# A graph transformer block: the product of probabilities and values, split into two matmuls of 64 columns

## The reference

```
q = q.reshape(B, T, H, HD) * HD ** (-0.5)
...
att = jax.nn.softmax(jnp.einsum('bthd,bshd->bhts', q, k), axis=-1)
o = jnp.einsum('bhts,bshd->bthd', att, v).reshape(B, T, D)
```

## Time and profile before

| | |
|---|---|
| runs of the kernel | 1949.89 and 1949.10 us, median 1949.49 |
| profiled execution, span from the first to the last instruction | 1945.8 us |
| instructions in it | 30993 |
| TensorE busy | 1816.8 us, 93% |
| VectorE busy | 1184.2 us, 61% |
| ScalarE busy | 722.9 us, 37% |
| attention stage, products of probabilities and values | from 499.8 to 1664.1 us |

### The profile page before, as it was taken

The page is one execution under the profiler, slowest core; times in us unless marked ns, Lnnn a source line. Parts: engine busy times, 40 slices in busy tenths (PEclk is TensorE's granted clock), DMA queues, the critical chain, the costliest instruction groups (busy, mean ns, idle before and its releaser), DMA issues.

```text
span 1945.8 us, 30993 instructions
## 1 busy us (share of the span) xinstructions
PE 1816.8 (93%) x10495; PEld 1626.1 (84%) x10495; DVE 1184.2 (61%) x2343; ACT 722.9 (37%) x1346; POOL 337.8 (17%) x335
## 2 busy tenths in 40 slices
PE   2999989987899999999999999989999999899998
PEld 1788567855899999999889898889999999787996
DVE  7776568775566546663756747656566666675332
ACT  1223201014555445445544553245555444220110
POOL 3210001002112112020101003100000013565440
PEclk9999999988899999999999999999999999999999
DMA  3101001011021100030000000000000002111111
GB/s 109 33 7 44 11 11 33 1 48 44 12 118 33 28 28 6 1 123 12 12 6 12 12 1 17 23 11 12 6 12 6 7 1 68 51 59 44 44 33 53
DMA packets 24782, 58.00 MB, mean 30 GB/s; under 512 B 2537, under 2 KB 4805, under 8 KB 24013
## 3 DMA queue, kind: packets, MB, share of 16 engines
q1 hardware_dynamic: 24650, 56.18, 8.9%
HBM read 44.87 MB, written 11.30 MB: 29 GB/s over the span
## 4 chain that ended last, share of the span: by engine, by line
PE 85%; DVE 7%; issue 2%; DMA 2%; DVEq 1%; POOL 1%; ACT 1%; SPq 0%; POOLq 0%; ACTq 0%
PE ps L2284 21%; PE ps L2169 13%; PE ps L2339 7%; PE ps L2227 6%; PE ps L2266 6%; PE ps L2270 6%; PE ps L1961 6%; PE ps L2368 4%; PE ps L2055 3%; PE ps L2092 3%; PE ps L1974 1%; PE ps L2295 1%; DVE share L1729 1%; DMA tok_a<-in_x 1%; DVE max_part L1712 1%
## 5 line engine op out<-in xcount | busy, mean ns | idle before, releaser
L2284 PE MATMUL ps<-p_raw,v_ones 125*128 125x250 f32 x2080 | 526.8, 375 | 9.7 <-DVE feat L1731 6.2
L1712 DVE TENSOR_REDUCE max_part<-ps 125x2 f32<-125x500 f32 x520 | 330.3, 674 | 213.6 <-PE ps L2227 203.2
L1288 ACT ACTIVATE p_raw<-ps 125x500 f32<-125x500 f32 x520 | 304.1, 586 | 332.0 <-PE ps L2270 327.5
L2284 PEld LDWEIGHTS ps<-p_raw,v_ones 125*128 125x128 f32 x2080 | 360.9, 190 | 36.2 <-issue 7.7
L1729 DVE RECIPROCAL share<-ps 64x250 f32<-64x250 f32 x120 | 206.2, 1718 | 86.1 <-PE ps L2284 83.5
L2266 PE MATMUL ps<-q_both_a,k_both_a 128*125 128x250 f32 x520 | 183.8, 374 | 1.8 <-issue 0.9
L2266 PE MATMUL ps<-q_both_b,k_both_b 128*125 128x250 f32 x520 | 181.7, 371 | 0.0
L1552 DVE TENSOR_SCALAR onehot<-iota_h,win_key,key_t 125x320 f16 x453 | 172.2, 380 | 0.7 <-issue 0.6
L892 POOL CAST w_hi<-w_raw 128x512 fp32r<-128x512 f32 x44 | 28.3, 642 | 816.7 <-issue 351.8
L2169 PE MATMUL ps<-xa_hi,w_hi 128*128 128x418 f32 (+1 forms) x448 | 151.1, 337 | 13.4 <-POOL w_lo L894 9.1
L1551 DVE TENSOR_SCALAR onehot<-iota_h,low_t 125x125 f16 x453 | 124.4, 275 | 57.8 <-PE ps L2092 29.2
(11 more groups left out here) (378 smaller groups left out, 3399.2 us busy)
## 6 DMA issues: line engine op xcount, KB each, us to landing
w_raw<-in_w_mlp SPq DMA_DIRECT2D x32, 256.0 KB, 2.6
w_raw<-in_w_gps SPq DMA_DIRECT2D x16, 256.0 KB, 2.6
w_raw<-in_w_tp SPq DMA_DIRECT2D x16, 256.0 KB, 2.6
w_raw<-in_w_sp SPq DMA_DIRECT2D x12, 256.0 KB, 2.6
w_raw<-in_w_cr SPq DMA_DIRECT2D x12, 256.0 KB, 2.6
d_xt<-xb_hi SPq DMA_DIRECT2D x1, 2508.0 KB, 7.4
d_xt<-xb_lo SPq DMA_DIRECT2D x1, 2508.0 KB, 14.9
xa_hi<-d_xt SPq DMA_DIRECT2D x1, 2508.0 KB, 9.7
```

The source lines that it names most:

```text
L1288: act.activation(p_raw[:, g % PR, :], ps[0:TOK, g % 2, 0:4 * TOK], ACT.Exp, scale=SCALE).then_inc(s_exp, 1)
L1712: dve.tensor_reduce(part[:, y, :, j], ps[0:TOK, bank, 0:4 * TOK].rearrange("p (h k) -> p h k", h=2), AX.X, ALU.max)\
L2284: ins = pe.matmul(ps[:, bank, 0:2 * TOK], v_ones[:, n % 2, kt, h:h + 2, :], p_raw[:, g % PR, cols], start=(b == 0 and x == 0), stop=last)
```

## The change

Each matmul of `product` becomes two. The first takes the group `h` as 64 columns and writes partitions 0 to 63 of the bank, the second the group `h + 1` and writes partitions 64 to 127. Both read the same 250 columns of `p_raw`. Each half starts and ends its own sum; the semaphore is raised by the last matmul, as before.

```
-                    ins = pe.matmul(ps[:, bank, 0:2 * TOK], v_ones[:, n % 2, kt, h:h + 2, :], p_raw[:, g % PR, cols], start=(b == 0 and x == 0), stop=last)
+                    for y in range(2):
+                        ins = pe.matmul(ps[64 * y:64 * y + 64, bank, 0:2 * TOK], v_ones[:, n % 2, kt, h + y, :], p_raw[:, g % PR, cols],
+                                        start=(b == 0 and x == 0), stop=last)
                 ins.then_inc(s_pv, 1)
```

## The result

The changed kernel takes 2110.61 us (2109.42 to 2111.81) against 1949.49: ratio 1.0831, 95% interval 1.0811 to 1.0852, so it is slower by 161 us. The forecast was 2250 us, with a range of 2100 to 2570: the direction held and the time lies in the range, but it lies where the rival "perfect overlap with excursions" stood (2105), not at the forecast itself.

A forecast was written before the change was run, and what follows sets the result against it. TensorE was taken to bound the kernel. Per product, 0.28 us for passes and 0.32 for changing width make 0.60, times 518 is 311 us; less 10 us of waits, from 1949.49 this gave 2250 us, range 2100 to 2570.

The forecast's parts named there:

- perfect overlap with excursions: Rival for the product: halves run fully side by side, each change of width costs 0.32 us; 2105 us, chance 0.09.
- 4 T: Lower bound of a product's passes: each half makes four passes of T = 0.21 us, both halves side by side.
- the staircase: Forecast case: a product's halves overlap only partly, in five pass times, 1.06 us; with excursions, chance 0.52.
- What bounds the kernel: Attention stage: TensorE sets the pace, busy 1197.11 of 1240 us; what is added to it is added to the time.
- Part 1, the passes: In each product, twice as many passes over half the columns: body from 0.85 to 1.13 us, +0.28.
- The allowance for late loads: In a product, first passes in a just freed half may wait for their weight load: 0 to 0.15 us, 0.07 taken.
- Part 2, the excursion: Around products, going from full-width matmuls into a half and out again: 0.32 us each, 518 times.
- The row that spoke against it: L2238, a transpose with 33 active columns between full-width matmuls, showed no standing still before or after.
- The sum: Whole kernel: 0.60 us a product, 518 times, 311 us, less 10 us for waits on max_col and feat; 2250 us.
- halves one after the other: Rival for the product: eight passes in turn, 1.70 us, plus excursions; 2545 us, chance 0.23.
- Not slower: Rival: excursions free for 64 columns, halves side by side all the time; product stays 0.85 us, kernel 1950 us, chance 0.05.
- The granted clock falls: Possible upward correction: clock at 0.95 instead of 0.99 makes some 1500 us of work 4% longer, +60 us; no own chance.

## Why the prediction was right, and where not

The direction and the range held; the central figure did not. 2250 us was 139 us too much, and the time lies near the lower end of the range (2100), which was set by the bound of 4 T. The case that came true, pairs from the first pass on with excursions, had a chance of 0.09, against 0.52 for the staircase.

*What bounds the kernel*: right. TensorE set the pace before and does so now; the other engines' busy times did not move, and the products now last from 499.9 to 1826.5 us, 162 us longer than before.

*Part 1, the passes*: wrong in its term of +0.28 us a product; it measured 0. Three things stood in it. That a narrower pass is no cheaper held: 1.90 us for eight in one half. That halves overlap held too; it was called an assumption there. The step that failed is "the two passes of one matmul use the same half, so they follow each other; the first pass of the upper half can start only beside the second of the lower half". It took the order of issue for the order of start across both halves. The run that issues one half wholly ahead of the other shows that this order binds within a half alone, so the body stays at the lower bound, 4 T. The allowance for late loads in it (0.07) fell away with the staircase; only the first load shows, and that was in the excursion's price already (the +0.06 above).

*Part 2, the excursion*: right in mechanism and in size. 0.32 was forecast from the bias row L1964; 0.34 is read from the trace of the changed kernel, and 0.311 is left of it in the time, 0.31 to 0.32 in three more kernels with 260, 520 and 976 excursions. The row that spoke against it was rightly set aside: the transpose was the exception.

The Trainium skill's rule on a change of the tiling mode ("TensorEngine Tiling (Array Packing)", Key Properties) is borne out by these runs: a change between full width and halves costs TensorE's time, 0.34 us for both ways, and going from one half to the other within a product costs nothing that the steps of 0.21 us show. Of the Trainium skill's "TensorE: Matmul & The Clock Gate", Part 3, the trace agrees that two column groups run together (1.07 us for eight passes); its statement that matmuls start and end strictly in program order doesn't fit the time of the run with one half issued ahead of the other, which is 1.07 us too.

*The sum*: 518 x (0 + 0.34) = 176 us, less some 15 us that came back, is the 161 us measured. The prediction took 10 us off for the waits on max_col and feat. Those two went from 7.9 and 6.2 only to 7.9 and 4.5; what came back came from elsewhere, so this term was short by some 5 us and stood in the wrong place. That the rival's 2105 comes within 6 us of the time is in part luck: its excursion was 0.02 too cheap, 10 us in all, and half of that is made up by what it took off too little.

*The rivals*: "halves one after the other" is out by 434 us, and the run with both in one half shows what it would have been (2529.52 measured, 2545 worked out). "Not slower" needed excursions that are free for 64 columns; the only narrow form that these runs show to be free is the float32 transpose with 33. "The granted clock falls" didn't happen: 0.99 in the stage.

## What to carry to other kernels

Splitting a full-width matmul into column halves gained nothing here, since both halves together do what one pass did, and each trip from full width into halves and back cost 0.34 us, 0.31 to 0.32 after what came back elsewhere: count the trips, not the matmuls. It follows, though no run here tried it, that halves can pay only where each has work of its own that would otherwise take a pass of its own, in stretches that are long against 0.34 us. A matmul of few rows or columns between full ones makes the same kind of trip, so padding it, here to 65 rows or 65 columns, can be the faster way (5.7 us in 1948).

## What the runs showed of the hardware

Each column half works off its own sequence: four passes of one half, issued ahead, don't hold up the other (1.07 us for eight in either order, 1.90 with all eight in one half). A trip from full width into halves and back costs 0.34 us, and the weight loads at both changes are not started ahead. A float32 transpose with 33 active columns stays out of the narrow way of working that a plain matmul of the same 33 columns goes into: 0.12 against 0.21 us from the L2270 ahead of it.
